# A fused window-attention, convolution and curvature-flow kernel: convolutions of a wave drawn forward, first half of the images moved and split earlier, stencil matrices brought by a casting transfer

## The reference

```python
x = _L0_conv_ref(x, ...)   # patch attention, then window attention; the last product is
                           # _merge(wf) @ Wout_w, of 1024 x 16384 weights; out + x
x = _L1_conv_ref(x, w1, b1, w2, b2)   # conv3x3, relu, conv3x3, + x
x = _L2_conv_ref(x, w1, b1, w2, b2)   # the same with other weights
x = _L3_conv_ref(x, alpha, beta)      # 10 steps of a curvature flow:

def step(u, _):
    ux, uy, uxx, uxy, uyy = _derivs(u)      # Sobel stencils, applied once and twice
    K = clip((uxx * uyy - uxy * uxy) / (denK * denK + EPS), -5, 5)
    H = clip(((1 + uy*uy)*uxx - 2*ux*uy*uxy + (1 + ux*ux)*uyy) / (2*denH**3 + EPS), -5, 5)
    u = u + DT * clip(alpha * K + beta * H, -1, 1)
    return pad(u[:, :, 1:-1, 1:-1], mode='edge'), None
return 0.7 * u + 0.3 * x
```

## Time and profile before

| | |
|---|---|
| median of 3 runs | 815.54 us (813.55 to 815.72) |
| profiled execution, its own time | 815.8 us |
| its span | 814.0 us |
| PE busy | 664.8 us (82%) |
| DVE busy | 460.5 us (57%) |
| ACT busy | 401.5 us (49%) |
| POOL busy | 273.0 us (34%) |
| HBM read | 164.99 MB |
| mean granted TensorE clock | 0.947 of full speed |

### The profile page before, as it was taken

How to read it: one execution, slowest core, us unless ns; L and a number is a source line. 1 busy time by engine, 2 the same in 40 slices (tenths; PEclk the granted TensorE clock), 3 DMA queues, 4 the chain that set the end, 5 groups by cost and what they waited for, 6 DMA issues and landing times.

```text
span 814.0 us, 11430 instructions
## 1 busy us (share of the span) xinstructions
PE 664.8 (82%) x4616; PEld 487.7 (60%) x4616; DVE 460.5 (57%) x626; ACT 401.5 (49%) x613; POOL 273.0 (34%) x239
## 2 busy tenths in 40 slices
PE   0799989799755659887899988888888888888882
PEld 0587735454322236565677767767767767776770
DVE  6740001930300212222244899999999999999995
ACT  1300001500000001121122899999999999999995
POOL 1000000000210600000011576676677677577672
PEclk9999999899976689899999999999999999999997
DMA  9949898998999999999950000000000000000001
GB/s 378 413 167 419 350 428 361 385 436 365 417 397 414 416 434 431 422 435 433 416 209 1 0 2 1 0 0 0 0 0 0 0 0 0 0 0 0 0 0 52
DMA packets 10993, 166.53 MB, mean 205 GB/s; under 512 B 1232, under 2 KB 1360, under 8 KB 5712
## 3 DMA queue, kind: packets, MB, share of 16 engines
q1 hardware_dynamic: 9744, 164.30, 48.2%
q10 hardware_dynamic: 672, 1.41, 0.5%
q0 software_dynamic: 544, 0.33, 0.1%
HBM read 164.99 MB, written 1.05 MB: 204 GB/s over the span
## 4 chain that ended last, share of the span: by engine, by line
DVE 30%; PE 27%; DMA 24%; POOL 11%; ACT 6%; issue 2%; POOLq 0%; DVEq 0%; SPq 0%; ACTq 0%
DMA ring<-wout_w 17%; PE bank L369 7%; PE bank L381 7%; POOL ring L1090 5%; POOL ring L1092 5%; DVE ring L818 5%; DVE ring L822 5%; DVE ring L830 5%; DMA ring<-wv_w 4%; PE bank L419 4%; PE bank L476 3%; DVE reg_b L835 3%; DVE ring L826 2%; DVE ring L839 2%; DVE reg_a L848 2%
## 5 line engine op out<-in xcount | busy, mean ns | idle before, releaser
L555 PE MATMUL bank<-u_parts,vmr 128*128 128x480 f32 x1360 | 305.2, 382 | 46.0 <-DVE ring L818 45.2
L555 PEld LDWEIGHTS bank<-u_parts,vmr 128*128 128x128 f32 x1360 | 252.6, 188 | 98.6 <-issue 48.0
L381 PE MATMUL bank<-ring,small 128*32 128x256 f32 x1152 | 82.1, 449 | 29.0 <-DMA ring<-wout_w 25.0
L1090 POOL TENSOR_TENSOR ring<-ring 128x480 f32<-128x480 f32 x40 | 49.1, 1227 | 105.0 <-DVE reg_a L848 80.1
L381 PEld LDWEIGHTS bank<-ring,small 128*32 128x32 f32 x1152 | 41.7, 128 | 65.2 <-DMA ring<-wout_w 32.5
L811 DVE TENSOR_SCALAR ring<-bank 128x1440 f32<-128x1440 f32 x40 | 66.0, 1650 | 4.5 <-PE bank L555 4.5
L790 DVE STREAM_TRANSPOSE reg_b<-bank 128x256 f32<-128x256 f32 x16 | 7.2, 449 | 106.0 <-PE bank L381 106.0
L369 PE MATMUL bank<-reg_a,ring 128*128 128x256 f32 x256 | 58.9, 394 | 3.6 <-ACT reg_a L894 3.6
L936 ACT ACTIVATE reg_e<-xa 32x384 f32<-32x384 f32 (+9 forms) x16 | 8.3, 521 | 107.5 <-DVE xa L793 81.2
L818 DVE TENSOR_TENSOR ring<-ring,bank 128x960 f32<-128x960 f32 x40 | 46.2, 1154 | 23.6 <-POOL ring L1092 23.6
L381 PE MATMUL bank<-ring,reg_e 128*32 128x256 f32 x512 | 38.3, 469 | 24.0 <-DMA ring<-wv_w 24.0
(11 more groups left out here) (185 smaller groups left out, 989.1 us busy)
## 6 DMA issues: line engine op xcount, KB each, us to landing
ring<-wv_w SPq DMA_DIRECT2D x16, 4096.0 KB, 26.3
ring<-wout_w SPq DMA_DIRECT2D x15, 4096.0 KB, 33.7
ring<-wqk_p SPq DMA_DIRECT2D x2, 4096.0 KB, 30.7
ring<-wqk_w SPq DMA_DIRECT2D x2, 4096.0 KB, 13.8
ring<-wv_p SPq DMA_DIRECT2D x1, 4096.0 KB, 13.5
ring<-wout_p SPq DMA_DIRECT2D x1, 4096.0 KB, 21.9
ring<-wout_w SPq DMA_DIRECT2D x4, 1024.0 KB, 30.8
ring<-vmats SPq DMA_DIRECT2D x1, 1664.0 KB, 6.1
```

The costliest lines, as they stand in the source:

```text
L381: ins = te.matmul(bank[32 * j:32 * j + 32, b_, n0:n0 + 256], lhs(c), slot[k % NSLOT][:, c, 256 * j:256 * j + 256], start=start and c == 0, ...
L555: last = te.matmul(dst[:, 0:NF], mat(m, first), p3[:, 2 + off:S + off, :], start=(high and n == 0), stop=(not high and n == len(terms) - 1))
L1090: p.tensor_tensor(abs_[n], ab[n][:, 0:NF], ab[n][:, NF:2 * NF], ALU.add).then_inc(po["absum"], 1)
```

## The change

Seven edits, in the order of time:

1. `convs_after`: layers 0 and 1 of the waves 0 to 2 both follow the slot that completes the wave (slots 3, 7, 11); layers 2 and 3 follow the next two slots. No convolution follows slot 14 any more. The last wave keeps its four layers after slot 15.
2. `chunk_rows` of half 0 follows slot 14 instead of slot 15. Its fourth chunk goes to PSUM bank 0, since bank 7 is slot 15's (`chunk_bank`). The first convolution of the last wave therefore waits for ACT's four copies (`ac["u_in"]`), which now stand ahead of that layer's halo copies on ACT.
3. The stencil matrices: SP's transfer into the ring and POOL's cast go. POOL issues one transfer from HBM straight into `vmr`, float32 to float32r, once slot 15 is used.
4. `edge_m`, needed only at the very end, has a semaphore of its own.
5. ACT rounds the first half of each chunk of u (272 columns) to `u_hi` after the last halo copy of the last convolution.
6. POOL computes the first half of `u_lo` once these four and all halo copies are done.
7. The rounding and subtraction at the start of the flow then cover the second half alone (272 columns instead of 544). PE waits for `ld_vm`, `hi_first` and `lo_first` ahead of the first stencil.

```diff
@@ convs_after
     if s == NO - 1:
         return [(WAVES - 1, layer) for layer in range(NCONV)]
-    return [(w, s - G + 1 - G * w) for w in range(WAVES - 1) if 0 <= s - G + 1 - G * w < NCONV]
+    return [(w, layer) for w in range(WAVES - 1) for layer in range(NCONV) if s == G * (w + 1) - 1 + max(layer - 1, 0)]
...
+def chunk_bank(x, half):
+    return 4 + x if half or x < NCH - 1 else 0
@@ sync
             sp.wait_ge(pe["slot_used"], U_ALL)
-            sp.dma_start(vm, vmats).then_inc(ld_vm, 16)
-            sp.dma_start(edge_m, edge).then_inc(ld_vm, 16)
+            sp.dma_start(edge_m, edge).then_inc(ld_edge, 16)
@@ tensor
-                if s_ == NO - 1:
+                if s_ == NO - 2:
                     te.wait_ge(po["pick"], 1)
                     te.wait_ge(ve["conv"], pairs_done(WAVES - 2, NCONV - 1, 1))
                     for x in range(NCH):
-                        te.wait_ge(ve["bank_turn"], NO + x + 1)
+                        te.wait_ge(ve["bank_turn"], NO + min(x, 2) + 1)
...
+                    if (w, layer) == (WAVES - 1, 0):
+                        te.wait_ge(ac["u_in"], NCH)
...
-            te.wait_ge(po["vm"], 1)
-            te.wait_ge(ld_vm, 32)
+            te.wait_ge(ld_vm, 16)
+            te.wait_ge(ac["hi_first"], NCH)
+            te.wait_ge(po["lo_first"], NCH)
@@ scalar
-                halo_rows(a, ...)
                 if (w, layer) == (WAVES - 1, 0):
...
+                halo_rows(a, ...)
+                if (w, layer) == (WAVES - 1, NCONV - 1):
+                    a.wait_ge(pe["slot_used"], U_ALL)
+                    a.wait_ge(ac["u_in"], NCH)
+                    for x in range(NCH):
+                        a.activation(u_hi[x][:, FIRST], u[x][:, FIRST], ACT.Copy).then_inc(ac["hi_first"], 1)
...
-                    a.activation(u_hi[c], u[c], ACT.Copy).then_inc(ac["hi"], 1)
+                    a.activation(u_hi[c][:, SECOND], u[c][:, SECOND], ACT.Copy).then_inc(ac["hi"], 1)
@@ gpsimd
-            p.wait_ge(ld_vm, 32)
-            p.tensor_copy(vmr[:, :], vm).then_inc(po["vm"], 1)
+            p.wait_ge(pe["slot_used"], U_ALL)
+            p.dma_start(vmr[:, :], vmats).then_inc(ld_vm, 16)
+            p.wait_ge(ac["hi_first"], NCH)
+            p.wait_ge(ac["halo"], 2 * WAVES * NCONV)
+            p.wait_ge(ve["halo"], 4 * WAVES * NCONV)
+            for x in range(NCH):
+                p.tensor_tensor(u_lo[x][:, FIRST], u[x][:, FIRST], u_hi[x][:, FIRST].bitcast(F32),
+                                ALU.subtract).then_inc(po["lo_first"], 1)
```

More of the change, by code:

```diff
@@ L189, in build @@
         ld_slot = [sem(f"ld_slot{r}") for r in range(NSLOT)]
-        ld_band, ld_vm = sem("ld_band"), sem("ld_vm")
+        ld_band, ld_vm, ld_edge = sem("ld_band"), sem("ld_vm"), sem("ld_edge")
         pe = {n: sem("pe_" + n) for n in (
@@ L202, in build @@
             "order", "patch_sq", "patch_std", "fl", "win_sq", "win_std", "pl_std", "qkv", "vt", "exp", "pt", "rows",
-            "wwk", "wv", "conv", "p2", "sqr", "lnw", "psq", "w15", "lnd", "inv", "low_end", "ends", "x3", "pad", "hi", "halo", "u_in")}
-        po = {n: sem("po_" + n) for n in ("zero", "stat", "bandz", "pick", "vm", "padz", "lo", "cxy", "m", "absum", "hn")}
+            "wwk", "wv", "conv", "p2", "sqr", "lnw", "psq", "w15", "lnd", "inv", "low_end", "ends", "x3", "pad", "hi", "hi_first", "halo", "u_in")}
+        po = {n: sem("po_" + n) for n in ("zero", "stat", "bandz", "pick", "padz", "lo", "lo_first", "cxy", "m", "absum", "hn")}
         ld_last, st_out = [sem(f"ld_last{n}") for n in range(NPIECE)], sem("st_out")
@@ L251, in build @@
         u_half = lambda c, half: u[c][:, B + half * HALF:B + (half + 1) * HALF]
-        vm = ring[:, la[0]:la[0] + NVM]
+        FIRST, SECOND = slice(0, B + HALF), slice(B + HALF, ROWF)
         fld = dual(5 * NF)
@@ L513, in chunk_rows @@
                 w0 = half * S // 2
-                return te.matmul(bank[QUAD * g:QUAD * (g + 1), 4 + x, (1 - half) * HALF:(2 - half) * HALF],
+                return te.matmul(bank[QUAD * g:QUAD * (g + 1), chunk_bank(x, half), (1 - half) * HALF:(2 - half) * HALF],
                                  pick[:, x * QUAD:(x + 1) * QUAD],
@@ L541, in _ @@
             te.wait_ge(ac["u_in"], NCH)
+            te.wait_ge(ve["bank_turn"], NO + NSLOT)
             for h in range(2):
@@ L586, in _ @@
                     fields(i * NCH + (c + 1), c, False, True)
+            te.wait_ge(ld_edge, 16)
             for x in range(NCH):
@@ L935, in _ @@
                 a_, b_ = columns(w, layer)
-                halo_rows(a, lambda o, i: a.activation(o, i, ACT.Copy), (0,), w, layer, halo_source(layer),
-                          halo_waits(w, layer), ac["halo"])
                 if (w, layer) == (WAVES - 1, 0):
@@ L941, in _ @@
                         a.wait_ge(pe["chunk"], x + 1)
-                        a.activation(u_half(x, 0), bank[:, 4 + x, HALF:2 * HALF], ACT.Copy).then_inc(ac["u_in"], 1)
+                        a.activation(u_half(x, 0), bank[:, chunk_bank(x, 0), HALF:2 * HALF], ACT.Copy).then_inc(ac["u_in"], 1)
+                halo_rows(a, lambda o, i: a.activation(o, i, ACT.Copy), (0,), w, layer, halo_source(layer),
+                          halo_waits(w, layer), ac["halo"])
+                if (w, layer) == (WAVES - 1, NCONV - 1):
[3 more added lines that the diff above has]
+                        a.activation(u_hi[x][:, FIRST], u[x][:, FIRST], ACT.Copy).then_inc(ac["hi_first"], 1)
                 if layer % 2:
@@ L1069, in _ @@
             p.memset(reg_g[:, :], 0.0).then_inc(po["padz"], 1)
-            p.wait_ge(ld_vm, 32)
-            p.tensor_copy(vmr[:, :], vm).then_inc(po["vm"], 1)
+            p.wait_ge(pe["slot_used"], U_ALL)
[6 more added lines that the diff above has]
+                                ALU.subtract).then_inc(po["lo_first"], 1)
             def low(k, c, later=True):
                 p.wait_ge(ac["hi"], k)
-                at = slice(B, (S + 1) * B) if later else slice(0, ROWF)
+                at = slice(B, (S + 1) * B) if later else SECOND
                 p.tensor_tensor(u_lo[c][:, at], u[c][:, at], u_hi[c][:, at].bitcast(F32),
```

## The result

Shared rounds on one chip gave the changed kernel 811.5 us (median of 5 runs, 810.41 to 812.47) and the kernel before 815.72 us (5 runs, 813.55 to 817.07). The ratio is 0.995, with a 95% interval of 0.9935 to 0.9966: faster by 2.8 to 5.3 us. The forecast was 812.1 us in a range of 810.6 to 815.0. Four of all the executions in this document, three of the kernel before and one of edits 5 to 7, took 972 us or more and are left out of the ratios.

The account below looks back on a forecast made before the run. It took the weight stream, then PE's chain in the tail up to the first stencil, to bound the kernel. Terms 1.3 + 1.7 + 0.4 = 3.4 us took the profiled 815.8 to 812.4, median 812.1 us; range 810.6 to 815.0.

Parts of the forecast that it names:

- The front: Start of the tail, edits 1 and 2: the last wave's first layer starts at 417.3 instead of 418.66, -1.3 us.
- the spare time: PE's slack before slot 15: 1.6 us ahead of slot 14, 1.6 us more ahead of the last piece, 3.2 in all.
- the last quarter: Part of slot 15's `thin` that needs the stream's last piece: 0.92 us, ending at 416.4 instead of 416.93.
- The cast: Last wave's halo copies, edits 3 and 4: without POOL's cast the halo matmuls no longer wait for DVE's copies, -1.7 us.
- The split: Flow's second and third slot steps, edits 5 to 7: half-width roundings on ACT's chain, -0.4 us.
- B: Last slot: POOL's issue gets in DVE's way, price 1.5 us, giving 813.6 us; chance 0.10.
- C: Before the first stencil: the casting transfer lands late and stencils wait for `ld_vm`, giving 818.1 us; chance 0.09.
- my two ends: Bounds for the casting transfer's time: 6.1 us from SP's same bytes, 144 us at the pace of small POOL transfers.
- the estimate of 5.9 us: Casting transfer's time by the skill's fit for a GpSimd transfer, 2.0 us and 436 GB/s.
- D: Ahead of slot 15's end: last piece lands earlier or early layers free more, 1.5 us more, 810.6 us; chance 0.08.
- E: Weight stream bounds everything before the last wave, so edits 1 and 2 give nothing: 813.4 us; chance 0.08.
- A: Near the last wave: PE's clock falls after new idle time, one fall costs 1.7 us, giving 813.8 us; chance 0.15.

Follow-up runs that it names:

- late cast: Changed kernel with edits 3 and 4 undone and POOL's cast put off until all halo copies are done: 812.8 us (12 runs), ratio 0.9974.

## Why the prediction was right, and where it was off

**The front (predicted -1.3 us): right, -1.1 us.** In the changed kernel PE was idle for 5.9 us ahead of slot 11, which then took 6.57 us, and the spare time swallowed it, as foreseen; nothing was left of it ahead of slot 14, and 0.83 us ahead of the last piece. PE in time's order, slots 11, 12, the two parts of slot 15, and the last wave's first layer:

```profile
374.41 6.57 PE L386 MATMUL bank<-ring,small 128*32 128x256 f32 x64 [5.90 <-DMA ring<-wout_w]
...
389.61 3.66 PE L386 MATMUL bank<-ring,small 128*32 128x256 f32 x64
...
409.82 2.77 PE L386 MATMUL bank<-ring,small 128*32 128x256 f32 x48
413.42 1.07 PE L386 MATMUL bank<-ring,small 128*32 128x256 f32 x16 [0.83 <-DMA ring<-wout_w]
415.38 3.21 PE L507 MATMUL bank<-xa,reg_c 128*128 128x144 f32 x24 [0.90 <-DVE xa L803]
```

The wait for DVE is the 0.90 us of the earlier trace rows exactly. The main mis-sized piece is the last quarter: I took 3.66 / 4 = 0.92 us, it took 1.07. Cut at a wait, the 64 matmuls take 2.77 + 1.07 = 3.84 us instead of 3.66. The two traces of edits 1 and 2 alone show the whole term (first layer 2.0 us behind the landing). Apart, edit 1 gives 0.35 us of it and edit 2 costs 1.6 us.

**The cast (predicted -1.7 us): right in size, wrong as a term by itself.** Against before, layers went from 25.2 to 23.3 us, -1.9. But I added this to the front as if the two were independent. They aren't: edit 2 brings the copies 0.8 us forward, and in both traces of edits 1 and 2 the cast then comes too late to hold any of them up. In the traces' tails edits 1 and 2 take off 3.0 us, edits 3 and 4 alone 2.2, and the changed kernel, which has both, 3.0 and not 5.2. In the third kernel with edit 2's order and the cast (the changed one without edits 3 and 4) the cast did meet the second copy, and edits 3 and 4 are worth 1.8 us there (27.1 to 25.3). So beside edit 2 the transfer gains 1.8 us in some executions and nothing in others. How often, no run shows: the medians have it at 0.4 us in the same rounds (812.12 to 811.7), which is within their noise. Without edit 2 the second copy starts some 8.0 us behind slot 15's end, later than any of the seven casts, so there the collision is sure. This is why the sum holds all the same: it sets a kernel in which cast and copies collide against one without a cast. What fails is the share of each edit: most of the 1.9 us can come from edit 2 already.

Had I laid the cast's start (7.2 us behind slot 15) on the forecast order of the copies, I would have found it within tenths of a microsecond of the start of their second one, and called it a coin toss.

The Trainium skill, "SBUF — State Buffer", section "Who interferes with whom", says that whoever issues first holds the shared ports for the whole instruction. The held copies agree: each came second and lasted until just behind the cast's end, 0.34 us behind it (427.41 against 427.07 before, not the cast's end itself as I had read it). That POOL is held in turn isn't shown. The cast took 2.96 to 3.08 us in all seven traces, whether it began during a copy or not, and 2.96 us where it met none; but spans on POOL are rough.

**The split (predicted -0.4 us): right, -0.3 us**, from 370.2 to 369.9 or 370.0 us of flow. That is below what timing resolves; only the traces show it, but they do so each time: six without the split have a flow of 370.2 or 370.3 us, five with it 369.9 to 370.1. It lies where it was forecast: DVE's first clips of slot steps two, three and four start 9.67 and 8.93 us apart before and 9.44 and 8.79 us in the changed kernel. The new work is hidden as foreseen. POOL's subtractions, in time's order, end at 435.76, 2.9 us ahead of the first stencil (predicted 3):

```profile
432.81 2.22 POOL L1093 TENSOR_TENSOR u_parts<-reg_a,u_parts 128x272 fp32r<-128x272 f32 x3 [17.43 <-ACT u_parts L958]
435.00 0.76 POOL L1093 TENSOR_TENSOR u_parts<-reg_g,u_parts 128x272 fp32r<-128x272 f32 x1
```

**The sum**: 3.3 us by the traces against 3.4 forecast, both with the head left out. The medians fell by 4.2 us, 0.8 more than forecast. None of my terms makes that up; the head, which I left out, moves by more than that from one execution to the next.

**The rivals.** B is wrong: POOL's issue took 0.57 us at 414.82, and DVE's transpose and addition beside it took 0.45 and 0.29 us as always. C is wrong: 7.1 and 7.4 us to land, with 23.8 us of cover; of my two ends, 6.1 and 144 us, the row of the same size was the right one, and the estimate of 5.9 us beside it was short by 1.2 to 1.5 us. D and E are wrong: the stream is as long in every kernel. A is right as a mechanism, absent from both traces of the changed kernel, seen in one trace of nine with its front, at 1.5 us where I had 1.7.

## What to carry to other kernels

To move work from behind the last landing to ahead of it, first take something else away there, so that it has room: neither edit paid alone. When a change moves one of two instructions of which one holds up the other, work out both start times again before adding up the terms; a collision that costs 2 us may hang on a few tenths. And compare traces from the last event that the change can't touch: here 2.1 us of a 5.4 us difference in span stood there before it.

## What was not expected of the hardware

- A POOL cast of 2.96 us held up the next DVE copy that came while it ran, until 0.34 us behind its own end, but not the copy that was under way when it began (480 ns). A pair of copies took 0.99 us with the cast beginning during its second copy, and 3.50 us with it beginning 0.3 us ahead of that one.
- DVE instructions on 128x2 elements took 0.70 us instead of 0.17 beside POOL subtractions of about 0.75 us each.
- A transfer that casts float32 to float32r, 1664 KB from POOL's queue, landed in 7.1 to 7.4 us in six traces, against 6.1 us for the same bytes without a cast on SP's queue.
- Behind nearly the same work and waits of PE, the granted clock fell to 0.50 in one execution and stayed at 1.00 in another. That was seen twice, in the last wave's first layer (late cast against edits 1 and 2) and in its third (edits 5 to 7 against before). What decides it stays open.
